# A pre-norm transformer layer on one core: one load, the lead of the row maxima and one bias addition moved by a few slots of a hand-written order

## The chip, the cores and the metric

The kernel runs on one NeuronCore of a Trainium2 chip. The metric is the device time of one execution in microseconds (us). The kernel before takes 2010.45 us, the median of 3 runs from 2010.45 to 2010.8.

## The reference

The input x has the shape (4, 2048, 256) in float32. The layer is attention and then a linear layer, each behind a layer norm and with a residual:

```
x = x + attention(layernorm(x))       # 16 heads of 16, causal, scores / sqrt(256), @ Wo + bo
x = x + linear(layernorm(x))          # weight 256 x 256, + bias
```

In the linear layer both operands are quantised first, in blocks of 32 along a row: each block is divided by its largest magnitude / 7.5, every value goes to the nearest point of the 6-bit grid E2M3, and the block is multiplied by its scale again.

## The kernel before

The tokens are cut into 16 chunks of 512 (four to a batch, n = 0 to 15). The heads are taken in groups of four: 4 batches x 4 groups of heads are 16 groups, and a group has four quarters k = 4g + qc, one for each chunk of 512 queries. A *step* of a quarter is one block of 128 keys against its 512 queries, so the quarters have 4, 8, 12 and 16 steps, a group has 40 and the kernel NS = 640. One *slot* p is the time of one step. Every engine runs a program of its own, in order, and the engines meet only at semaphores; each program is a loop over the same slots, from -20 to about 653.

In slot p TensorE (PE) computes the scores of step p for four heads (`scores`, split in four strips of 32 columns by `by_columns`, L1447), ScalarE (ACT) takes their exponential (L1031), GpSimd (POOL) masks the triangle of a step on the diagonal (`mask`, L840), and PE multiplies by the values two slots later (`values`, L1488). The diagonal steps come early in a quarter and are narrower: 512, 384, 256 and 128 columns.

The exponential needs the maximum of each row beforehand. So PE computes the scores of a quarter once more, ahead of time and the other way round (`unit`, L1447 too): 128 queries against up to 512 keys, into a ring of four PSUM banks, which VectorE (DVE) reduces (`take_unit`, L1189; on the diagonal the masked form of L1184). `max_steps_until(p)` says how many steps of maxima are done by slot p: in the steady part it is p + `MAX_LEAD`, with a ramp in the opening. When a quarter's maxima are all there (slot `MAX_DONE[k]`), four operations follow, a slot apart: `maximum` on DVE (L1196), `split_max` on POOL (L877 to L881, in three bfloat16 parts), `turn_max` on SP (L687, a DMA transpose) and `load_max` on SP (L694, three DMAs into rows 96 to 98 of `q_rows`, so that the score matmul subtracts the maximum itself). The quarter's first score waits for these rows.

Around this stand two other kinds of work, both put into slots by a planner of a few lines at the head of the file. `put` takes the first slot from p on in which the engine has room, by costs written at each call.
- *Projection* of a chunk (`place_early` for chunks 0 to 3, `place_project` for the others, which starts at slot 160 b + 4 + 30 c): `load_x` brings 512 KB of x, DVE takes statistics, POOL (for chunks 0 to 3 DVE) normalises, PE transposes and multiplies by Wq, Wk, Wv, POOL splits Q and K in three bfloat16 parts (L861 to L869), SP stores them to HBM (`store_qk`, four a chunk, numbered r = 4n + m; `store_v`). `load_rows(g, c)` then brings a chunk's rows of Q and K for one group with twelve DMAs of 64 KB (L674), once the four stores of that chunk are in. Chunk 4's `load_x` is followed on SP by `load_later_weights`: Wo, the linear layer's weight and the two biases broadcast over the partitions, four DMAs of 256, 256, 128 and 128 KB.
- *Output* of a chunk, in two halves a = 0, 1 (`place_output`), once all four groups of heads of its batch are done: SP loads the sums (`load_ctx`), the inverses of the denominators (`load_inverse`) and x (`load_again`, 512 KB, L768). POOL adds the first bias to x (`add_mid_bias`, L893) and multiplies the sums by the inverses (`weigh`, L888), PE multiplies by Wo (`attend`), DVE adds the result to x (L1229), and a chain of norm, block maxima, rounding and the second matmul (`feed`) follows. The last four chunks ("late", `quick`) are not weighed but turned on PE (`turn_ctx`).

The order within one slot is fixed in each engine's loop. On SP it is `turn_max`, `load_max`, `store_ctx`, `store_qk`, `store_v`, `load_x`, `load_rows`, `load_values`, and then the output's DMAs, `load_again` last. On POOL it is `mask`, `split_max`, the projection's work, then `weigh` and the output's other work, with `add_mid_bias` last. DVE takes the slot's maxima in four shares with the projection's and the output's work between them.

Of the kernel before, what the change touches and what calls it, by code (L numbers as in the profile page):

```python
# [19 lines left out]
QC = C // CHUNK  # L20
# [36 lines left out]
FIRSTS = [sum(SIZES[:k]) for k in range(NK)]  # L57
# [24 lines left out]

COLUMNS = 32
PRO = 20
MAX_LEAD = 21
SLOTS = range(-PRO, NS + 200)


def max_steps_until(p):

    if p < 0:
        return max(0, min(4, 2 * (p + PRO - 11))) + max(0, min(8, 2 * (p + PRO - 15)))
    if p < 7:
        return 12 + (p + 1) * 12 // 7
    if p < 20:
        return 24 + (p - 6) * 17 // 13
    return min(NS, p + MAX_LEAD)


UNITS_AT = {p: [n for m in range(max_steps_until(p - 1) if p > -PRO else 0, max_steps_until(p))  # L100
                for n in UNIT_STEPS[m]] for p in SLOTS}
MAX_DONE = [min(p for p in SLOTS if max_steps_until(p) >= FIRSTS[k] + SIZES[k]) for k in range(NK)]


# [22 lines left out]
def spend(engine, p, cost):  # L127
    FILLED[engine, p] = FILLED.get((engine, p), 0) + cost
# [10 lines left out]
def item(p, cost, *what):  # L139
    return put("items", p, cost, *what)  # L140


def vector(p, cost, *what):
    return put("vector", p, cost, *what)


def pool(p, cost, *what):
    return put("pool", p, cost, *what)


def sync(p, kind, *which):
    AT.setdefault((kind, p), []).append(which)
# [7 lines left out]
def late(n):  # L160

    return n >= NCH - QC
# [23 lines left out]


def place_project(n, start):
    sync(start - 6, "load_x", n)
    p = vector(start + 1, 0.85, "stats", n, 0)  # L190
    p = vector(p, 0.85, "stats", n, 1)
    p = vector(p, 0.65, "moments", n)
    p = pool(p + 1, 1.0, "deviation", n)
    for a in range(2):
        p = pool(p, 1.2, "normal", n, a)
    p += 1
    for e in range(EH):
        p = item(p, 0.45, "turn_x", n, e)
    p += 2
    lows = []  # L200
    for m, j in ((0, None), (1, 0), (2, None), (3, 1)):

        p = item(max(p, lows[m - 2] if m > 1 else p), 1.75, "project", n, m)
        r = 4 * n + m
        q = pool(p + 2, 1.7, "split", r)
        q = pool(q, 1.7, "split_low", r)
        lows.append(q)
        sync(q + 1, "store_qk", r)
        if j is not None:
            p = item(p + 1, 1.75, "project_v", n, j)  # L210
        p += 1
    sync(max(p, q) + 1, "store_v", n)
    return max(p, q) + 1


def after(p):

    return p + 1 if p < TAIL else p
# [6 lines left out]
def in_order(stage, p):  # L225
    return max(p, STAGE.get(stage, p))


def by_rows(k):


    return k < NK - QC * QC


def place_output(n, a, p):

    quick = late(n)

    def by_vector(p, cost, kind):
        STAGE[kind] = vector(in_order(kind, p), cost, kind, n, a)  # L240
        return STAGE[kind]

    def by_pool(p, cost, kind):
        STAGE[kind] = pool(in_order(kind, p), cost, kind, n, a)
        return STAGE[kind]

    def by_items(p, cost, kind):
        STAGE[kind] = item(in_order(kind, p), cost, kind, n, a)
        return STAGE[kind]

    mid_biased = by_pool(p, 1.35, "add_mid_bias")
    p = by_items(p, 0.45, "turn_ctx") if quick else by_pool(p, 1.3, "weigh")
    p = by_items(max(p + 1 + (p < TAIL), mid_biased), 1.95, "attend")
    spend("vector", p + 1, 0.7)
    p = by_vector(p + 1, 0.85, "stats2")
    p = by_vector(p, 0.35, "moments2")
    p = by_pool(after(p), 1.0, "deviation2")
    p = by_vector(after(p), 1.0, "quick_normal2") if quick else by_pool(p, 1.2, "normal2")
    p = by_vector(p if quick else p + 1, 0.65, "block_max")
    p = by_vector(p, 0.4, "scale")  # L260
    p = by_vector(p, 0.6, "quick_divide") if quick else by_pool(p + 1, 1.3, "divide")
    p = by_vector(p if quick else p + 1, 0.4, "exponent")
    p = by_vector(p, 0.4, "shift_high")
    p = by_vector(p, 0.4, "shift_low")
    q = by_pool(after(p), 1.35, "odd")
    q = by_pool(q, 1.35, "odd_back")
    if quick:
        p = by_vector(p, 0.6, "quick_even")
        p = by_vector(p, 0.6, "quick_even_back")
    else:  # L270
        q = by_pool(q, 1.35, "even")
        q = by_pool(q, 1.35, "even_back")
    p = by_vector(max(p, after(q)), 0.6, "grid")
    p = by_vector(p, 0.6, "quick_dequantise") if quick else by_pool(p + 1, 1.3, "dequantise")
    out_biased = by_pool(q if quick else p, 1.35, "add_out_bias")
    p = by_items(after(p), 0.45, "turn_xd")
    p = by_items(max(p + 1 + (p < TAIL), out_biased), 1.95, "feed")
    spend("vector", p + 1, 0.7)
    sync(p + 2, "store_out", n, a)
    return p + 2  # L280
# [28 lines left out]
for k in range(NK):  # L309
    p = vector(MAX_DONE[k], 0.3, "maximum", k)  # L310
    p = pool(p + 1, 0.9, "split_max", k)
    sync(p + 1, "turn_max", k)
    sync(p + 2, "load_max", k)
    assert p + 4 <= FIRSTS[k] or k < 1, (k, p, FIRSTS[k])
    done_at = FIRSTS[k] + SIZES[k] + 1
    if by_rows(k):
        STORED[k] = p = done_at + 1
        sync(p, "store_ctx", k)
        if k // QC % QC == QC - 1:
            n = k // (QC * QC) * QC + k % QC  # L320
            sync(p + 2, "load_den", n)
            p = vector(p + 7, 0.6, "invert", n) + 1
            sync(p, "store_inverse", n)
            INVERTED[n] = p
        continue
    TURNED[k] = item(done_at + 1, 0.45, "turn_acc", k)
    spend("vector", TURNED[k] + 1, 0.7)
    if k < NK - QC:
        STORED[k] = TURNED[k] + 2
        sync(STORED[k], "store_ctx", k)  # L330
# [4 lines left out]
for b in range(B):  # L335
    if b + 1 < B:
        for c in range(QC):
            n = QC * (b + 1) + c
            PROJECTED[n] = place_project(n, 160 * b + 4 + 30 * c)
            assert PROJECTED[n] + 3 < 160 * b + 138 + 6 * c, (n, PROJECTED[n])  # L340
    for c in range(QC):
        n = QC * b + c
        k = (QC * (b + 1) - 1) * QC + c
        before, times = before_in_set(n)
        free = 0
        if before is not None:
            free = DONE_AT[before] + 1
        elif out_set(n) == 1:
            free = max(PROJECTED.values()) + 2
        if late(n):  # L350
            load = max(STORED[k - QC] + 2, NS - GROUP_STEPS + 2 if before is None else READ_AT[before] + 2)
            ready = max(TURNED[k] + 1, load + 2)
        else:
            load = max(INVERTED[n] + 2, free)
            sync(load, "load_inverse", n)
            ready = load + 5
        sync(load, "load_ctx", n)
        sync(max(load, free), "load_again", n)
        ready = max(ready, free)
        ends = [place_output(n, a, ready) for a in range(2)]  # L360
        READ_AT[n], DONE_AT[n] = STAGE["turn_ctx" if late(n) else "attend"], ends[-1]
for g in range(NG):
    for c in range(QC):
        p = max(GROUP_STEPS * (g - 1) + (8 if g == 1 else 2) + 3 * c, -PRO)
        n = QC * (g // QC) + c
        p = max(p, PROJECTED[n] + 1)
        sync(p, "load_rows", g, c)
        sync(max(p, GROUP_STEPS * (g - 1) + 5 + 3 * c), "load_values", g, c)
p = 36
for step in range(6):  # L370
    p = vector(p, 1.4, "weights", step)
# [1263 lines left out]
```

## Time and profile before

| | |
|---|---|
| median of 3 runs | 2010.45 us |
| the profiled execution | 2009.58 us |
| its span in the trace | 2007.6 us |
| slots 0 to 639 (first score to last) | 95.3 to about 1950 us, some 2.9 us a slot |
| busy share PE, DVE, ACT, POOL | 93%, 85%, 67%, 45% |
| mean granted clock of TensorE | 0.979 |

The page gives the busy time of each engine, the span in 40 slices, the chain of work that ended last and the costliest groups of instructions. The views of the trace used below are the list of waits (which engine waited for which, in total), the timelines of single engines, the chain in order of time, and the busy time by stretches. "[6.57 <-DMA k_rows]" at an instruction means that its engine sat idle for 6.57 us before it and that this transfer ended the wait. SPq is SP's queue of DMA issues. The granted clock is 1.00 at 2.4 GHz and 0.50 at 1.2 GHz.

### The profile page before, as it was taken

How to read it: one execution, taken by the hardware profiler on the slowest of the kernel's cores; microseconds unless marked ns; L12 is line 12 of the kernel's file. 1: busy time of each engine (PE TensorE's matmuls, PEld its weight loads, DVE VectorE, ACT ScalarE, POOL GpSimd, SP SyncE). 2: the span in 40 equal slices, each digit the busy share in tenths (PEclk: the TensorE clock that was granted, in tenths of full speed). 3: DMA queues.
4: the chain of work that ended last, by engine and by line, in shares of the span. 5: the costliest groups of instructions: out<-in, count | busy, mean ns of one | idle time of the engine just before them, and what ended most of it. 6: DMA issues, size and time to landing. Idle time of an engine off the chain costs nothing.

```text
span 2007.6 us, 72033 instructions
## 1 busy us (share of the span) xinstructions
PE 1865.3 (93%) x30053; PEld 801.3 (40%) x30053; DVE 1709.2 (85%) x4334; ACT 1337.6 (67%) x2817; POOL 897.6 (45%) x1187
## 2 busy tenths in 40 slices
PE   6689999999999999999999999999999999999883
PEld 2234444344334443444334343444434444444432
DVE  4697987979988979888897988888999999999976
ACT  5356676777766767677676767666766666777660
POOL 4323334232446546565254646555354654411343
PEclk9899999999999999999999999999999999999996
DMA  5433141414041231503323151331514040131000
GB/s 162 130 85 104 42 114 40 111 52 127 22 125 60 72 107 53 170 18 85 97 59 108 47 153 45 80 117 33 151 42 131 13 110 28 54 86 33 3 33 22
DMA packets 173621, 156.73 MB, mean 78 GB/s; under 512 B 43248, under 2 KB 161008, under 8 KB 173296
## 3 DMA queue, kind: packets, MB, share of 16 engines
q1 hardware_dynamic: 173296, 152.13, 26.9%
q8 instruction: 236, 3.87, 0.8%
q14 instruction: 89, 0.73, 0.1%
HBM read 92.14 MB, written 57.02 MB: 74 GB/s over the span
## 4 chain that ended last, share of the span: by engine, by line
PE 51%; DVE 29%; issue 5%; SPq 4%; POOL 4%; DMA 4%; ACT 2%; POOLq 0%; DVEq 0%; ACTq 0%
PE psum L1447 36%; DVE max_parts L1189 15%; PE psum L1488 13%; DVE psum L1184 6%; SPq L674 3%; ACT probs L1031 2%; DMA out_shop<-in_L_attn_x 1%; DVE max_parts L1184 1%; PE psum L1515 1%; DMA max_rows<-neg_max 1%; PE psum L1507 1%; DVE stats L1248 1%; DVE block_max L1319 1%; POOL out_shop L924 1%; DMA k_rows<-qk_scratch 1%
## 5 line engine op out<-in xcount | busy, mean ns | idle before, releaser
L1031 ACT ACTIVATE probs<-psum 128x512 f32<-128x512 f32 (+3 forms) x2560 | 1204.2, 539 | 422.4 <-PE psum L1447 407.4
L1189 DVE TENSOR_REDUCE max_parts<-psum 128x1 f32<-128x512 f32 x1536 | 956.3, 680 | 96.4 <-PE psum L1447 91.7
L1447 PE MATMUL psum<-q_rows,k_rows 99*32 99x512 bf16 (+3 forms) x10240 | 886.7, 351 | 17.8 <-ACT probs L1031 7.6
L1447 PE MATMUL psum<-k_rows,q_rows 96*32 96x512 bf16 (+3 forms) x10240 | 848.5, 352 | 56.3 <-DVE max_parts L1189 17.4
L1488 PE MATMUL psum<-probs,v_in 128*17 128x512 f32 (+3 forms) x5120 | 587.0, 533 | 4.4 <-POOL probs L840 4.0
L1184 DVE CUSTOM_DVE_ANT_0 psum<-psum,causal 128x128 f32<-128x128 f32 (+3 forms) x1024 | 475.0, 518 | 111.8 <-PE psum L1447 107.9
L1447 PEld LDWEIGHTS psum<-k_rows,q_rows 96*32 96x32 bf16 x10240 | 273.1, 97 | 451.5 <-DVE max_parts L1189 170.3
L1447 PEld LDWEIGHTS psum<-q_rows,k_rows 99*32 99x32 bf16 x10240 | 275.2, 96 | 427.9 <-ACT probs L1031 226.8
L840 POOL TENSOR_SCALAR_AFFINE_SELECT probs<-probs 128x512 f32<-128x512 f32 x256 | 165.9, 648 | 581.5 <-ACT probs L1031 580.5
L1488 PEld LDWEIGHTS psum<-probs,v_in 128*17 128x17 f32 x5120 | 143.3, 98 | 93.4 <-POOL probs L840 5.5
L1184 DVE DVE_READ_ACCUMULATOR2_ANT max_parts<- 128x1 f32 x1024 | 143.4, 140 | 0.0
L877 POOL CAST neg_max<-neg_rest 128x16 bf16<-128x16 f32 x64 | 12.9, 201 | 160.3 <-DVE neg_rest L1196 139.7
L1055 ACT COPY shop<-psum 128x512 f32<-128x512 f32 x56 | 32.9, 587 | 74.4 <-PE psum L1447 74.4
L893 POOL TENSOR_TENSOR out_shop<-out_shop,biases 128x512 f32<-128x512 f32 x48 | 63.2, 1318 | 34.3 <-DMA out_shop<-in_L_attn_x 34.2
L869 POOL TENSOR_TENSOR shop<-shop 128x512 bf16<-128x512 f32 x56 | 65.6, 1171 | 4.6
L1447 PE MATMUL psum<-shop,w_q 128*32 128x512 f32 x512 | 64.6, 632 | 1.6 <-DVE max_parts L1189 0.7
L1447 PE MATMUL psum<-w_v,shop 128*32 128x256 f32 x1024 | 62.9, 387 | 0.6 <-DVE max_parts L1184 0.4
L1447 PE MATMUL psum<-shop,w_k 128*32 128x512 f32 x512 | 60.8, 592 | 0.9 <-DVE max_parts L1184 0.6
L1229 DVE TENSOR_TENSOR out_shop<-psum,out_shop 128x512 f32<-128x512 f32 x48 | 33.1, 691 | 32.0 <-PE psum L1447 31.6
L950 POOL TENSOR_TENSOR out_shop<-out_shop 128x512 f32<-128x512 f32 x24 | 31.9, 1328 | 61.5 <-DVE out_shop L1355 61.5
L853 POOL TENSOR_SCALAR shop<-shop,moments,inv_dev 128x256 f32<-128x256 f32 x48 | 58.8, 1235 | 0.8
L862 POOL TENSOR_TENSOR shop<-shop 128x512 f32<-128x512 f32 x48 | 56.2, 1172 | 4.0
(150 smaller groups left out, 1229.4 us busy)
## 6 DMA issues: line engine op xcount, KB each, us to landing
q_rows<-qk_scratch SPq DMA_DIRECT2D x384, 64.0 KB, 2.6
k_rows<-qk_scratch SPq DMA_DIRECT2D x384, 64.0 KB, 2.6
qk_scratch<-shop SPq DMA_DIRECT2D x56, 384.0 KB, 3.2
sums_scratch<-acc_sb SPq DMA_DIRECT2D x48, 256.0 KB, 2.3
shop<-in_L_attn_x SPq DMA_DIRECT2D x19, 512.0 KB, 4.5
v_scratch<-shop SPq DMA_DIRECT2D x16, 544.0 KB, 4.3
v_in<-v_scratch SPq DMA_DIRECT2D x64, 136.0 KB, 2.5
out_shop<-in_L_attn_x SPq DMA_DIRECT2D x12, 512.0 KB, 7.9
```

The costliest lines, as they stand in the source:

```text
L674: sp.dma_start(dst, src[i if which else l]).then_inc(kq_loaded[u][c], 16)
L840: nc.gpsimd.affine_select(out=tri, in_=tri, compare_op=ALU.is_ge, fill=0.0, base=0, pattern=[[0, HG], [1, P]], channel_multiplier=-1).then ...
L853: ins = nc.gpsimd.tensor_scalar(x_in[n % 2][:, j, :], x_in[n % 2][:, j, :], moments[:, j, 0:1], inv_dev[:, j:j + 1], ALU.subtract, ALU.mult)
L862: nc.gpsimd.tensor_tensor(out=proj[v], in0=proj[v], in1=parts[v][:, 0, :], op=ALU.subtract).then_inc(rest_ready, 1)
L869: nc.gpsimd.tensor_tensor(out=parts[v][:, 2, :], in0=proj[v], in1=parts[v][:, 1, :], op=ALU.subtract).then_inc(low_ready, 1)
L893: return nc.gpsimd.tensor_tensor(out=mine, in0=mine, in1=biases[:, i:i + 1, :].broadcast_to([P, 2, E]), op=ALU.add)
L1031: nc.scalar.activation(probs[s % NPROBS][:, h, a:CHUNK], bank[SCORE_BANKS[n % 3]][:, a:CHUNK], ACT.Exp, scale=SCALE).then_inc(probs_ready, 1)
L1184: ins = nc.vector.tensor_tensor_reduce(out=mine, in0=mine, in1=causal[:, CHUNK - width:CHUNK], scale=1.0, scalar=LOWEST, op0=ALU.add, op1= ...
L1189: nc.vector.tensor_reduce(max_parts[k % 2][:, first:first + heads, t % TILES, c], ring_bank(UNIT_USE[n])[:, 0:heads * width] .rearrange("p ...
L1229: nc.vector.tensor_tensor(out=mine, in0=ring_bank(ITEM_USE[what, n, a]) .rearrange("p (j e) -> p j e", e=E), in1=mine, op=ALU.add).then_in ...
L1447: ins = nc.tensor.matmul(out[r:r + COLUMNS], weights[:, r:r + COLUMNS], moving, start=start, stop=stop)
L1488: ins = nc.tensor.matmul(psum[32 * h:32 * h + VW, ACC_BANK, a:CHUNK], v_in[u][:, kb, h * VW:(h + 1) * VW], probs[s % NPROBS][:, h, a:CHUNK ...
```

## The change

- `MAX_LEAD` goes from 21 to 23, and the ramp of the opening from 17/13 to 18/13 steps a slot so that it meets it. With it the assertion asks for six slots, not four, from a quarter's `split_max` on, except in the first group.
- `place_project` puts `load_x` no earlier than slot 2. Only chunk 4 was earlier (slot -2).
- `place_output` puts, for the chunks that are not late, `weigh` first and `add_mid_bias` two slots behind it. It was the other way round, with both asked for from the same slot on.

```diff
-MAX_LEAD = 21
+MAX_LEAD = 23
...
     if p < 20:
-        return 24 + (p - 6) * 17 // 13
+        return 24 + (p - 6) * 18 // 13
     return min(NS, p + MAX_LEAD)
...
 def place_project(n, start):
-    sync(start - 6, "load_x", n)
+    sync(max(start - 6, 2), "load_x", n)
...
-    mid_biased = by_pool(p, 1.35, "add_mid_bias")
-    p = by_items(p, 0.45, "turn_ctx") if quick else by_pool(p, 1.3, "weigh")
+    if quick:
+        mid_biased = by_pool(p, 1.35, "add_mid_bias")
+        p = by_items(p, 0.45, "turn_ctx")
+    else:
+        p = by_pool(p, 1.3, "weigh")
+        mid_biased = by_pool(p + 2, 1.35, "add_mid_bias")
     p = by_items(max(p + 1 + (p < TAIL), mid_biased), 1.95, "attend")
...
-    assert p + 4 <= FIRSTS[k] or k < 1, (k, p, FIRSTS[k])
+    assert p + (4 if k < QC else 6) <= FIRSTS[k] or k < 1, (k, p, FIRSTS[k])
```

## Rows read from the trace of the kernel before

**Rows 1.** The page: engines' busy us, share, instructions; the chain's shares by engine:
```profile
PE 1865.3 (93%) x30053; PEld 801.3 (40%) x30053; DVE 1709.2 (85%) x4334; ACT 1337.6 (67%) x2817; POOL 897.6 (45%) x1187
PE 51%; DVE 29%; issue 5%; SPq 4%; POOL 4%; DMA 4%; ACT 2%; POOLq 0%; DVEq 0%; ACTq 0%
```

**Rows 2.** Slots 120 to 159: engines in turn, granted clock, DMA share, GB/s:
```profile
450.60:469.80 19.20, 18.75 (x328) 7.61 (x324) 18.01 (x43) 14.88 (x35) 4.61 (x10) 1.00 0.35 87
469.80:495.70 25.90, 25.64 (x452) 11.03 (x448) 25.90 (x59) 20.21 (x48) 3.82 (x6) 1.00 0.58 152
495.70:551.40 55.70, 53.23 (x896) 21.40 (x892) 50.92 (x152) 41.11 (x84) 24.05 (x34) 1.00 0.12 34
```

**Rows 3.** Waits over the span: us in total, times, longest us:
```profile
POOL out_shop L893 <- DMA out_shop<-in_L_attn_x: 34.2, 6, 8.1
PEld psum L1447 <- DMA k_rows<-qk_scratch: 17.3, 3, 7.1
PE psum L1447 <- DMA q_rows<-max_rows: 5.7, 3, 3.7
PE psum L1488 <- POOL probs L840: 4.0, 2, 2.3
```

**Rows 4.** SP's timeline, opening: start us, duration us, what is issued:
```profile
87.36 0.49 SPq L645 DMA_DIRECT2D shop<-in_L_attn_x  x1
90.24 1.26 SPq L674 DMA_DIRECT2D q_rows<-qk_scratch  x3
112.34 0.42 SPq L674 DMA_DIRECT2D k_rows<-qk_scratch  x1
```

**Rows 5.** Chain of waits, opening: start us, duration us, what:
```profile
69.00 2.55 DMA k_rows<-qk_scratch
95.37 6.13 DMA k_rows<-qk_scratch
```

**Rows 6.** Timelines of PE and DVE, opening; idle time before in brackets:
```profile
101.55 0.62 PE L1447 MATMUL psum<-k_rows,q_rows 96*32 96x512 bf16 x4 [6.57 <-DMA k_rows<-qk_scratch]
121.97 0.75 DVE L1248 BATCH_NORM_STATS2 stats<-shop 128x6 f32<-128x256 f32 x2
130.41 0.69 DVE L1189 TENSOR_REDUCE max_parts<-psum 128x1 f32<-128x512 f32 x1
```

**Rows 7.** Twelve heads on the chain; masked maxima by shape (busy, mean ns):
```profile
470.38 7.12 DVE max_parts L1189 x12
L1184 DVE CUSTOM_DVE_ANT_0 psum<-psum,causal 128x512 f32<-128x512 f32 x256 | 170.2, 718 | 14.8 <-PE psum L1447 13.8
L1184 DVE CUSTOM_DVE_ANT_0 psum<-psum,causal 128x128 f32<-128x128 f32 x256 | 66.7, 322 | 46.0 <-PE psum L1447 45.7
```

**Rows 8.** Chain of waits: 13 heads on PE; one step of values:
```profile
730.67 2.84 PE psum L1447 x52
853.60 0.86 PE psum L1488 x8
```

**Rows 9.** Around slot 304: PE's timeline, the chain, POOL's timeline:
```profile
982.54 0.40 PE L1447 MATMUL psum<-q_rows,k_rows 99*32 99x512 bf16 x4 [3.69 <-DMA q_rows<-max_rows]
972.68 6.78 DMA max_rows<-neg_max
977.83 1.28 POOL L893 TENSOR_TENSOR out_shop<-out_shop,biases 128x512 f32<-128x512 f32 x1 [5.18 <-DMA out_shop<-in_L_attn_x]
```

**Rows 10.** Busy time by stretch around one wait for a mask:
```profile
850.00:852.00 2.00, 2.00 (x28) 0.96 (x32) 0.80 (x2) 0.56 (x2) 2.00 (x2) 0.50 0.34 119
852.00:854.00 2.00, 2.00 (x28) 0.73 (x20) 1.90 (x5) 1.20 (x2) 2.00 (x3) 0.67 0.00 1
844.00:848.00 4.00, 3.78 (x68) 1.44 (x59) 3.96 (x12) 3.23 (x8) 0.00 (x0) 1.00 1.04 347
```

**Rows 11.** Chunk 3's first addition: the chain, POOL's timeline:
```profile
839.32 8.55 DMA out_shop<-in_L_attn_x
848.01 1.26 POOL L893 TENSOR_TENSOR out_shop<-out_shop,biases 128x512 f32<-128x512 f32 x1 [7.60 <-DMA out_shop<-in_L_attn_x]
```

## The prediction

> **What bounds the kernel now.** I read the busy shares first: PE is busy 93% of the span and DVE 85% [rows 1]. The chain that ended last splits 51% PE, 29% DVE, 4% DMA, 4% POOL [rows 1]. So PE sets the pace, DVE takes it over in places, and a few waits for transfers stand between. In slots 120 to 159, a group of 40 slots with little other work, the three stretches of slots 0-7, 8-19 and 20-39 of the group show where which engine leads: in the middle one DVE is busy for all 25.9 us; in the last one it has 4.8 us to spare [rows 2]. Next the list of waits over the whole span [rows 3]: PE's weight loads wait 17.3 us for the rows of K (three times), its matmuls 5.7 us for the rows of the maxima and 4.0 us for masks, and POOL sits 34.2 us before the first bias's addition. POOL's idle time counts only where PE waits for a mask that stands behind it. The change touches exactly these three, and shifts the maxima against the scores.
>
> **Part 1, the load of chunk 4.** `load_x(4)` is the only one that moves: its slot was 4 - 6 = -2 and becomes 2; for the others start - 6 is far over 2. With it go the four DMAs of `load_later_weights`. On SP the five are issued from 87.36 on, and at 90.24 the twelve DMAs of `load_rows(0,2)` follow [rows 4]. The chain of waits names the landing of a store as what released the rows at 90.24. But that store is r = 13, of chunk 3, and `load_rows(0,2)` waits only for r up to 11; SP simply issues without a gap, so the five cost their issue time, 90.24 - 87.36 = 2.9 us. Their bytes cost as much again: the last K row of chunk 2 takes 6.13 us to land, where the same DMA of chunk 1 took 2.55 [rows 5]. PE sits 6.57 us for it [rows 6]. Without the five in front the row lands 2.9 + 3.6 = 6.5 us sooner, near 95.0, when PE has just come there; I take 6.4, all on the path, since DVE then runs without a gap for 40 us. Bounds: 0 (were the chain right, and the stores what makes the landing slow) and 7.0 (DVE's gap too).
> The load now passes the stores of r = 14 and 15, `turn_max(1)`, `store_v(3)` and `load_max(1)`, and stands before `load_rows(0,3)`. SP issued the last DMA of `load_rows(0,3)` at 112.34 [rows 4]. Five issues (2.9 us) and a landing 3.6 us longer put its end at 112.3 + 2.5 + 6.5 = 121.3 at the latest. The first maxima that need chunk 3 are taken by DVE at 130.41, now 124.0, so the cover is at least 2.7 us, and more by what SP too comes sooner; the statistics of chunk 4 at 121.97, now 115.6, need x that would be issued by 106 and even with 6 us lands before [rows 6]. I take nothing for either; if the cover were gone, what is late would come off the 6.4.
>
> **Part 2, the lead.** Two steps more by slot 20, and the last two slots with maxima (618 and 619) become free. Two early steps (256 and 384 columns, four heads) are 1.1 us on PE (2.5 x 4 x 0.215 / 2) or 3.6 on DVE (4 x 0.38 + 4 x 0.52 [rows 7]); two of 512 columns at the end are 1.7 us on PE (8 x 0.215 [rows 8]) or 5.0 on DVE (4 x 0.59 + 4 x 0.65). PE on both sides: -0.6. Bounds +1.9 and -3.9.
> *The wait for the rows of maxima.* It falls on the first slot of a group's last quarter, where only four slots stand between the last maxima and the first use. At slot 304 PE waits 3.69 us [rows 9], at slots 144 and 624 the other 2.0 of its 5.7 [rows 3]. After a wait of this kind PE runs at half the clock for a while: behind the mask's wait at 849.9 the granted clock is 0.50 (1.2 GHz) for 2 us and 0.67 for 2 more, 1.0 + 0.66 = 1.7 us lost [rows 10]; the same is lost behind slot 304. With two slots more (4.3 us, a sixth of the 25.9 us that 12 slots take) the first idea is that all of it goes, 5.7 us and 1.7 of clock, 7.4. The rows speak against that for slot 304. The transpose issued at 972.68 lands 6.78 us later, at 979.46; x of `load_again(4)`, issued 2.7 us before it, lands just before POOL's addition at 977.83 [rows 9]: the transpose is held by what was issued ahead, not only by the late maximum. `load_again(4)` is in slot 136 of its batch and still ahead of `turn_max`. Issued as soon as x is, at 970.9, the transpose lands after x all the same, near 978.2, and the wait falls by 1.3 us, not by 3.7, and the clock falls as before.
> The Trainium skill, page "DMA: Bandwidth & Descriptors", section "Queues, rings and completion order", says the same in general: the increment of a DMA's semaphore lands only after every earlier write of that DMA engine. By that rule a transpose behind x can't report before x; without it the gain at slot 304 would be the whole 3.7 and 1.7 of clock, and the sum would be 4.1 us lower, an estimate from the rows.
> I take 1.3 at slot 304, the 2.0 of the other two and 0.3 for what its weight loads lose besides: -3.6. Bounds 0 and -7.4.
> *How maxima and scores stand beside each other.* DVE needs for a head of 512 columns 0.59 us (12 in 7.12), for a masked one of 512 columns 0.65 and of 128 0.25 (0.07 less than the means, since starts overlap), for 384 and 256 columns 0.52 and 0.38 between them [rows 7]. PE needs 0.215 us for a head of 512 columns of scores or maxima (13 in 2.84, less a little), and 0.86 for a step of values [rows 8], less in proportion on the diagonal. Summed over a group by the kernel's own lists of steps, slots 0-7, 8-19, 20-39: lead 21 PE 17.2, 25.4, 45.1 and DVE 18.0, 26.4, 41.9; lead 23 PE 17.2, 24.7, 45.8 and DVE 18.0, 25.1, 43.1. The larger of the two in each stretch sums to 89.5 before and 88.9 after: 0.6 us a group, because full steps of maxima leave the short diagonal slots in the middle. The trace agrees on which engine leads where [rows 2]. Over 14 groups 8.4 us; projections and output work fill many of these gaps, so I take half, -4.2. Bounds: -8.4, and +14.4, if the 1.2 us more of DVE in slots 20-39 counts in full in the 12 groups that have output work.
>
> **Part 3, the first bias's addition.** For chunks 0 to 11 `weigh` now comes first and the addition two slots later. The addition is what waits for x, six times, 34.2 us. PE feels two of them, 4.0 us for masks, the longer 2.3 [rows 3]: for chunk 3 near 849.9 and, in the same place of the next batch, for chunk 7. POOL shows why: the addition starts at 848.01 after 7.60 us idle and takes 1.26 [rows 11], and the mask comes behind it. Both are followed by the low clock, 1.7 us each [rows 10]. Now `weigh` stands there and waits for the sums and the inverses, issued just ahead of x, which is issued at 839.32 and lands 8.55 us later [rows 11]. The trace doesn't show when they land. The 512 KB of x at the 347 GB/s of 844-848 take 1.5 us [rows 10], so at least that much earlier. The waits are 1.7 and 2.3, so at most 0.2 and 0.8 us stay, and I take both as gone: 4.0 + 3.4 = -7.4. Bounds 0 and -7.9 (0.5 that the weight loads wait besides). Nothing is added: the same 24 additions, and DVE's addition of `attend` waits for them as before.
>
> **Sum.** -6.4 - 0.6 - 3.6 - 4.2 - 7.4 = -22.2. The profiled execution took 2009.58 (span 2007.6 and 2.0 around it), so 1987.4; it lay 0.9 below the median of the runs, 2010.45, so 1988 in the runs.
>
> **Rivals.**
> *A, the waits only change their name.* `weigh` waits for the same full queue and the masks behind it with it, of the waits for the maxima's rows only 2.1 go, and the pairing gives nothing: -6.4 - 0.6 - 2.1 = -9.1, 2001. For it: 1 MB lies ahead of x in the same queue. Against it: PE needs only 2 us.
> *B, slower: DVE waits for the late addition.* `attend` is now two slots behind `weigh`, and DVE, in order, takes it one slot later and needs the addition. From `weigh` that is one slot (2.5) and the matmuls of `attend` (1.7), 4.2 us; POOL has the other half's `weigh` to do (the addition's kind and shape, 1.3 [rows 11]), a mask (0.65 on the page) and the addition, 3.2 us. It decides once one more POOL instruction of over 1.0 us stands between, as parts of the splits do (1.17 on the page). Everything behind on DVE, the maxima, then waits, and PE after four banks. At a whole addition for each of 24 halves: 24 x 1.28 = 30.7 on top of the sum, 2019.
> *C, all of it comes*: -7.0 - 3.9 - 7.4 - 8.4 - 7.9 = -34.6, 1976. For it: every term is a wait or a surplus that the rows show. Against it: the transpose behind x.
> *D, the gains are taken back*: what PE no longer waits for a transfer it waits for DVE, which is busy 85% itself [rows 1], or the change doesn't reach the waits at all: 2009.5 to 2010.5. Against it: PE's own idle time shows them.
>
> **Numbers.** Forecast 0.45, C 0.20, A 0.15, B 0.10, D 0.10. A measurement tells about 0.2% (4 us) from no change. Faster: 0.45 + 0.20 + 0.15 = 0.80; same 0.09; slower 0.11. The range reaches over A and to C and leaves B and D out: 1975 to 2006. The forecast's own is 1981 to 1997.
>
> **What would show it.** The last K row of chunk 2 lands near 95.0, in about 2.5 us, and PE's gap of 6.6 us before it is gone. `load_rows(0,3)` makes nobody wait. POOL's waits for x before the addition are gone or short, `weigh` has some of them, and no wait of PE for a mask stays, nor half clock behind it. At slot 304 a wait of 2 us or more for the maxima's rows stays with the transpose landing right after x; if it is gone, my reading of the queue is wrong. A group of 40 slots with little other work takes about 0.6 us less than 100.8. DVE waiting for POOL's addition would be B.

## The result: slower, not faster

The changed kernel takes 2018.8 us, the median of 11 runs, against 2007.3 for the kernel before on the same chip. The ratio is 1.0048, with a 95% interval from 1.0033 to 1.0064: +9.6 us, where -22 was forecast. The profiled execution took 2017.14 us with a span of 2015.4, 7.6 us more than that of before (2009.58). A profile shows one execution, and those of one kernel differ by up to 20 us here (2007.3 is the middle of 1998.0 to 2018.1), so the traces tell where time goes, and only the medians how much.

### The profile page after: what moved, and what is told of

Read it like the earlier page. It is cut to its first block, busy times and chain, and to the rows that moved or that the text cites. A ratio compares the mean times of both kernels' runs of the same rounds, so it can differ in the third digit from the quotient of the medians.

```text
span 2015.4 us, 72025 instructions
## 1 busy us (share of the span) xinstructions
PE 1869.2 (93%) x30053; PEld 804.0 (40%) x30053; DVE 1715.4 (85%) x4334; ACT 1332.4 (66%) x2817; POOL 892.8 (44%) x1187
## 4 chain that ended last, share of the span: by engine, by line
PE 60%; DVE 23%; issue 5%; ACT 5%; DMA 2%; SPq 2%; POOL 2%; POOLq 0%; DVEq 0%; ACTq 0%
PE psum L1452 42%; PE psum L1493 16%; DVE max_parts L1194 10%; DVE psum L1189 5%; ACT probs L1036 3%; SPq L679 2%; ACT acc_sb L1045 1%; DMA max_rows<-neg_max 1%; DVE max_parts L1189 1%; PE psum L1520 1%; PE psum L1512 1%; DVE out_shop L1355 1%; DVE block_max L1324 0%; DMA qk_scratch<-shop 0%; DVE stats L1253 0%
## 5 line engine op out<-in xcount | busy, mean ns | idle before, releaser
L1452 PE MATMUL psum<-q_rows,k_rows 99*32 99x512 bf16 (+3 forms) x10240 | 892.5, 351 | 26.8 <-ACT probs L1036 17.5
L1452 PE MATMUL psum<-k_rows,q_rows 96*32 96x512 bf16 (+3 forms) x10240 | 851.7, 351 | 42.4 <-DVE max_parts L1194 14.9
L1493 PE MATMUL psum<-probs,v_in 128*17 128x512 f32 (+3 forms) x5120 | 590.2, 533 | 13.9 <-POOL probs L845 9.6
L1452 PEld LDWEIGHTS psum<-q_rows,k_rows 99*32 99x32 bf16 x10240 | 278.2, 96 | 461.5 <-ACT probs L1036 249.2
L1452 PEld LDWEIGHTS psum<-k_rows,q_rows 96*32 96x32 bf16 x10240 | 273.2, 97 | 411.5 <-DVE max_parts L1194 146.6
L845 POOL TENSOR_SCALAR_AFFINE_SELECT probs<-probs 128x512 f32<-128x512 f32 x256 | 166.4, 650 | 589.3 <-ACT probs L1036 589.0
L1493 PEld LDWEIGHTS psum<-probs,v_in 128*17 128x17 f32 x5120 | 143.3, 98 | 102.0 <-POOL probs L845 11.9
L882 POOL CAST neg_max<-neg_rest 128x16 bf16<-128x16 f32 x64 | 12.7, 198 | 146.6 <-DVE neg_rest L1201 135.5
L1452 PE MATMUL psum<-shop,w_q 128*32 128x512 f32 x512 | 66.1, 644 | 0.7 <-ACT shop L1049 0.7
L1452 PE MATMUL psum<-shop,w_k 128*32 128x512 f32 x512 | 61.7, 593 | 1.8 <-DVE max_parts L1189 1.1
L898 POOL TENSOR_TENSOR out_shop<-out_shop,biases 128x512 f32<-128x512 f32 x48 | 62.7, 1314 | 0.2 <-DMA out_shop<-in_L_attn_x 0.2
L1452 PE MATMUL psum<-w_v,shop 128*32 128x256 f32 x1024 | 61.9, 382 | 1.0 <-DVE max_parts L1194 0.6
```

The costliest lines, as they stand in the source:

```text
L845: nc.gpsimd.affine_select(out=tri, in_=tri, compare_op=ALU.is_ge, fill=0.0, base=0, pattern=[[0, HG], [1, P]], channel_multiplier=-1).then ...
L898: return nc.gpsimd.tensor_tensor(out=mine, in0=mine, in1=biases[:, i:i + 1, :].broadcast_to([P, 2, E]), op=ALU.add)
L1452: ins = nc.tensor.matmul(out[r:r + COLUMNS], weights[:, r:r + COLUMNS], moving, start=start, stop=stop)
L1493: ins = nc.tensor.matmul(psum[32 * h:32 * h + VW, ACC_BANK, a:CHUNK], v_in[u][:, kb, h * VW:(h + 1) * VW], probs[s % NPROBS][:, h, a:CHUNK ...
```

## The profile after

All lines behind the planner stand five further down: L1447 is L1452, L1488 is L1493, L840 is L845, L674 is L679. Mind L893: it was the first bias's addition, and is now `weigh`; the addition is L898.

The page first (engines' busy us and shares; the chain's shares), beside [rows 1]:

```profile
PE 1869.2 (93%) x30053; PEld 804.0 (40%) x30053; DVE 1715.4 (85%) x4334; ACT 1332.4 (66%) x2817; POOL 892.8 (44%) x1187
PE 60%; DVE 23%; issue 5%; ACT 5%; DMA 2%; SPq 2%; POOL 2%; POOLq 0%; DVEq 0%; ACTq 0%
```

Nothing there says slower. The list of waits does (us in total, times, longest), beside [rows 3]:

```profile
POOL out_shop L893 <- DMA out_shop<-inverse_scratch: 64.9, 7, 15.0
PEld psum L1452 <- DMA k_rows<-qk_scratch: 11.3, 3, 5.4
PE psum L1493 <- POOL probs L845: 9.6, 6, 4.7
PE psum L1452 <- DMA q_rows<-max_rows: 6.0, 2, 3.6
```

PE's weight loads wait 6.0 us less for rows of K; PE waits as long as before for the maxima's rows, and 5.6 us more for masks. POOL, which sat 34.2 us before the addition, sits 64.9 us before the weighing.

*The opening came as forecast.* The timelines of PE and SP, with `load_x(4)` and the last row of chunk 3 [rows 4, 6]:

```profile
96.15 0.40 PE L1452 MATMUL psum<-k_rows,q_rows 96*32 96x512 bf16 x4 [0.26 <-DMA k_rows<-qk_scratch]
...
103.11 0.59 SPq L650 DMA_DIRECT2D shop<-in_L_attn_x  x1
...
112.04 0.43 SPq L679 DMA_DIRECT2D k_rows<-qk_scratch  x1
```

And the landing of chunk 2's last K row in the chain [rows 5]:

```profile
93.52 2.59 DMA k_rows<-qk_scratch
```

It lands at 96.1, not 101.5 (95.0 was forecast), and the gap of 6.57 us is 0.26. Slot 12 begins at 137.7, not 143.4.

*Then it is lost, in several places.* A slot begins here with its first exponential on ACT. Counted so, the changed kernel takes 3.7 us more than before in slots 20 to 39, 3.0 in 120 to 139, 2.8 in 300 to 319 and 6.2 in 460 to 479. Slots 240 to 279 take 8.0 us less, but 280 to 299 take 9.7 more, because the planner has moved work from the former to the latter; from 260 to 299 the net is 3.4 more, and in their copy, 420 to 459, 4.0. Slots 200 to 219 and 360 to 379 take 5.4 and 5.2 more, of which 3.2 come back each time in the next 20.

The longest waits for a mask stand in those last two stretches, at slot 218 and its copy in the next batch, 378: slots 211 to 239 take 93.9 us, before 89.3. SP's timeline ahead of it in the changed kernel (start, duration, what is issued):

```profile
706.57 2.96 SPq L679 DMA_DIRECT2D q_rows<-qk_scratch  x3
...
713.32 0.43 SPq L679 DMA_DIRECT2D k_rows<-qk_scratch  x1
713.85 0.37 SPq L686 DMA_DIRECT2D v_in<-v_scratch  x1
714.31 1.36 SPq L740 DMA_DIRECT2D out_shop<-sums_scratch  x2
715.77 1.21 SPq L767 DMA_DIRECT2D out_shop<-inverse_scratch  x2
717.02 0.47 SPq L773 DMA_DIRECT2D out_shop<-in_L_attn_x  x1
```

The same x in the kernel before:

```profile
716.99 0.45 SPq L768 DMA_DIRECT2D out_shop<-in_L_attn_x  x1
```

Both belong to slot 211. That slot begins at 698.5 after and at 704.3 before. PE had gained 5.8 us by then, and SP nothing: it is 18.5 us behind the slot instead of 12.7. Among what it has to issue first are, at 704.82 and 705.29, the last two stores of chunk 8, which the planner has moved from slot 192 to 209. What follows on POOL and PE:

```profile
723.77 1.26 POOL L893 TENSOR_TENSOR out_shop<-out_shop 128x512 f32<-128x512 f32 x1 [13.89 <-DMA out_shop<-inverse_scratch]
724.99 0.64 POOL L845 TENSOR_SCALAR_AFFINE_SELECT probs<-probs 128x512 f32<-128x512 f32 x1
...
725.68 1.05 PE L1493 MATMUL psum<-probs,v_in 128*17 128x256 f32 x8 [3.51 <-POOL probs L845]
```

And the busy time by stretch (length; PE, PEld, DVE, ACT, POOL; granted clock, DMA share, GB/s):

```profile
724.00:728.00 4.00, 2.32 (x40) 1.34 (x44) 0.58 (x5) 0.45 (x2) 3.77 (x8) 0.60 0.35 128
728.00:732.00 4.00, 4.00 (x48) 1.87 (x44) 1.23 (x7) 0.69 (x2) 3.92 (x5) 0.54 0.05 9
```

POOL waits 13.9 us for the inverses, the mask stands behind `weigh`, and PE waits 3.5 us for it. It starts again at 725.68 and works at a granted clock of 0.50 (1.2 GHz) until 731.7, which costs 6.0 / 2 = 3.0 us more; the 0.60 above is a mean with PE's idle time before 725.68 in it. One wait of 3.5 costs 6.5. The wait that the change removed at chunk 3 [rows 10, 11] has come back a chunk earlier, twice as long.

## The experiments

Medians in us, with the ratio to the kernel before (run beside it each time) and its interval.

| kernel | median | ratio | 95% |
|---|---|---|---|
| e1 load only | 2001.5 | 0.9966 | 0.9946 to 0.9986 |
| e2 lead only | 2028.7 | 1.0101 | 1.0075 to 1.0126 |
| e3 bias only | 2004.2 | 0.9987 | 0.9970 to 1.0003 |
| e4 lead and bias | 2024.3 | 1.0076 | 1.0050 to 1.0101 |
| e5 load and bias | 2003.0 | 0.9974 | 0.9963 to 0.9985 |
| e6 maxima early | 2024.4 | 1.0078 | 1.0056 to 1.0099 |
| e7 places only | 2034.4 | 1.0125 | 1.0105 to 1.0145 |
| e8 lead 22 | 2033.9 | 1.0123 | 1.0104 to 1.0142 |
| e9 late projections | 2010.8 | 1.0015 | 1.0003 to 1.0028 |
| e10 lead, early projections | 2029.1 | 1.0110 | 1.0093 to 1.0127 |
| e11 lead, rows spaced | 2015.0 | 1.0034 | 1.0019 to 1.0049 |
| e12 load, rows spaced | 1995.0 | 0.9943 | 0.9923 to 0.9962 |
| e13 the change, rows spaced | 2002.1 | 0.9975 | 0.9960 to 0.9991 |
| e14 load and bias, rows spaced | 1999.6 | 0.9961 | 0.9943 to 0.9980 |
| e15 load, rows 4 apart | 1998.8 | 0.9955 | 0.9935 to 0.9975 |

**Which part.** e1 to e4 are the diff's parts: e1 the line of `load_x`, e2 `MAX_LEAD` and the ramp, e3 the block of `place_output`, e4 the last two together. e5 has all but the lead.

> Only the load of chunk 4 moves. In the changed kernel slot 1 came 6.8 us sooner, and by slot 21 only 4.3 us of it were left. Theory T (the load is a gain, something else in the change is the loss): 3 to 7 us faster than before, PE's gap before the maxima of chunk 2 gone (6.6 to about 0), and the gain lasts past slot 21, since no maxima are added there. Rival R1 (an opening gain is taken back later by transfers or DVE whatever else is changed): less than 1.5 us faster.

> Only the lead goes to 23, with its ramp. Theory L (the planner moves projections and output work when the maxima move, and the new places are worse): 5 to 12 us slower than before, spread over the groups that have projections and output work. Rival W (the loss sits in weigh standing first, before the inverses land): no slower than before, -8 to 0 us, as the prediction's own terms say (-0.6 - 3.6 - 4.2).

> Only weigh first and the first bias's addition two slots later. Rival W: 8 to 15 us slower than before, POOL idle before weigh for the inverses 50 us or more in total and PE waits for masks of 4 us or more in each of two places. Theory L: -4 to +2 us; POOL's idle time for the inverses near the 34 us that it had for x, and PE's waits for masks at most the 4.0 us of before.

> The change without the moved load. If the load is worth what the opening showed, this is 3 to 7 us slower than the whole change, so 12 to 17 us slower than before. If the lead and the bias add up, it is the sum of the two kernels that have them alone; theory X (each is harmless alone, but together slot 216 comes 7 us sooner against loads that are issued no sooner, so POOL waits 14 us with a mask behind it): both alone within 4 us of before, this one 10 us or more slower, with the waits of 3.5 and 4.7 us for masks at slots 218 and 378 in this kernel and in neither of the other two.

> The kernel before with the load of chunk 4 and the first bias's addition moved, the lead left at 21. Theory L (the loss is all the lead's; the other two add up): -6.8 of the load alone and -2.6 of the bias alone, so 2008.6 - 9.4 = 1999, ratio 0.995. Rival X (the parts disturb each other, since the load and the addition change what POOL and SP do at other places): not faster than the load alone, 2001.5 or more, ratio 0.9966 or above.

By the ratios the load brings -6.8, the bias -2.6, the lead +20.3; the sum is +10.9, the whole change +9.6. So the lead is the whole loss. e2 is slower than either of its two cases had it, and e4 (+15.3) fell where the load's gain put it. e5, 5.2 us faster than before, falls on the rival's side by its number, but its interval overlaps that of the load alone: beside the load, the bias brings nothing that can be told.

**The lead itself, or the places that the planner finds with it?** With a lead of 23 the planner also puts the other work elsewhere: DVE's room in a slot hangs on `UNITS_AT`, and `split_max` takes POOL's room two slots earlier. Worked out from `put` for the lead alone, the last store of chunk 8's projection goes from slot 192 to 208, of chunk 9's from 229 to 245, of chunk 10's from 255 to 270. e6 keeps all places and moves only the maxima and their four operations; e7 keeps those (but for three quarters late in the kernel, where they lie a slot earlier) and moves the rest; e8 is one lead in between.

```
 # e6: behind the planner, which has run with a lead of 21
+MAX_LEAD, RAMP = 23, 18
+UNITS_AT = {...}; MAX_DONE = [...]
+...   (takes the old entries of the four kinds out of the plan)
+for k in range(NK):
+    for i, kind in enumerate(("maximum", "split_max", "turn_max", "load_max")):
+        sync(MAX_DONE[k] + i, kind, k)
 # e7: the same lines with 21, 17, behind a planner that has run with 23
 # e8
-MAX_LEAD = 21
+MAX_LEAD = 22
```

> The plan of the kernel before is kept slot by slot for projections, output work and loads; only the steps of maxima, maximum, split_max, turn_max and load_max take the places that a lead of 23 gives them. Nothing is left out. Theory P (what costs is that the planner, seeing the maxima two slots earlier, puts projections and output work elsewhere, at 214-216 instead of 211-215 and so on): about 2008.6 less what the wait for the rows of maxima brings, -3 to -6, so 2003 to 2006. Rival M (what costs is the maxima themselves beside the scores, as the 1.2 us more of DVE in slots 20-39 of a group): most of the 20 us of the lead alone, 2020 to 2029.

> The reverse: steps of maxima, maximum, split_max, turn_max and load_max stay where a lead of 21 has them; projections and output work lie where the planner puts them for a lead of 23. Theory P: nearly all the loss of the lead alone, 2022 to 2030. Rival M: near the kernel before, 2006 to 2012. If each does half, both kernels lie near 2018 and the two costs are independent.

> Lead 22 instead of 21, the early steps as before. The short (masked) steps of maxima now stand beside the short steps of scores instead of beside the long ones. If the loss of the lead grew with its size (theory of a smooth cost, rival M in its simple form): half of 20, 2018. If it hangs on where the planner puts the work (theory P): anything, since the places change again. If the pairing of short with long was worth what the sums over a group say, it is slower than both neighbours: over 2029.

Neither theory holds alone: +16 and +25 can't be halves of +20. Each of the two loses by itself. For e6 the trace shows one place: the planner had fitted the maxima's operations and the rest round each other, and now `split_max(11)`, `deviation` and a `normal` stand together in slot 98, and PE waits 4.3 us for the mask behind them at slot 101; slots 100 to 119 take 8.4 us more. (The profiled execution of e6, 2015.96, is its fastest, 8.5 us under its median, so the trace doesn't hold the whole loss.) So these kernels price a misfit too, not the lead alone. That lead 22 is as slow as 23 says that the cost does not grow with the lead. The number lies where the pairing's case put it, but the planner has moved the other work here as well, so that doesn't show the pairing.

**The end of the projections?** The whole difference in e9 and e10 is the start of the projections of batches 2 and 3.

```
-            PROJECTED[n] = place_project(n, 160 * b + 4 + 30 * c)
+            PROJECTED[n] = place_project(n, 160 * b + (5 if b else 4) + 30 * c)   # e9; e10: 3, with the lead of 23
```

> The kernel before (lead 21) with the start of the projections of batches 2 and 3 one slot later (5 instead of 4), batch 1 as it was. The planner's first-fit then ends chunk 8 at slot 208 instead of 192 and chunk 9 at 238 instead of 229 (12 and 13 likewise), as it does, nearly, for a lead of 23 (208 and 245); maxima and output work stay in their slots. Theory Q (the lead costs because first-fit lets the projections end up to 16 slots later, so that SP issues their stores and the rows behind them just ahead of the loads of x): slower by 6 to 15 us, 2015 to 2024. Rival M2 (the ends of the projections don't matter; what costs is the maxima's chain among the masks and normals of POOL): 2006 to 2011.

> Lead 23 as in the lead alone, with the start of the projections of batches 2 and 3 one slot earlier (3 instead of 4): chunks 8 and 12 end at 195 and 355 instead of 208 and 368; chunk 9 stays at 245. Theory Q: part of the 20 us comes back, 4 to 10, so 2019 to 2025. Rival M2: as the lead alone, 2026 to 2030.

A miss. Chunk 8 at 208 and chunk 9 at 238 together cost 3 us; chunk 8 back at 195 under the lead of 23 gives nothing. What neither run isolates is chunk 9's last store at slot 245, where the lead puts it, just ahead of `load_rows(7, 1)`.

**SP's lateness.** In e2 SP issues chunk 3's x 19.9 us after its slot, 251, begins at 826.6; before it was 10.0. SP's, POOL's and PE's timelines of e2 there:

```profile
846.46 0.45 SPq L768 DMA_DIRECT2D out_shop<-in_L_attn_x  x1
...
854.17 1.26 POOL L893 TENSOR_TENSOR out_shop<-out_shop,biases 128x512 f32<-128x512 f32 x1 [12.87 <-DMA out_shop<-in_L_attn_x]
...
856.07 1.06 PE L1488 MATMUL psum<-probs,v_in 128*17 128x256 f32 x8 [6.04 <-POOL probs L840]
```

Ahead of it SP issues the rows of four chunks, 48 DMAs, in slots 242 to 251, with the waits for their stores between. They aren't needed until the next group's maxima, from slot 257 on. e11 to e13 spread them:

```
-        p = max(GROUP_STEPS * (g - 1) + (8 if g == 1 else 2) + 3 * c, -PRO)
+        p = max(GROUP_STEPS * (g - 1) + (8 if g == 1 else 2) + 5 * c, -PRO)
```

> Lead 23 as in the lead alone, with the loads of K's and Q's rows of a group's four chunks 5 slots apart instead of 3 (slots 2, 7, 12, 17 of a group instead of 2, 5, 8, 11). All else as in the lead alone. There SP issued x of chunk 3 19.9 us after its slot had begun (10.0 in the kernel before), behind 24 DMAs of rows, and PE waited 13.0 us for masks with the half clock behind it. Theory Q: SP is no longer behind at slot 251, the wait of POOL for x and those of PE for masks are nearly gone, -10 to -16, so 2013 to 2019. Rival M2: SP's lateness isn't what delays the masks, 2025 to 2030.

> The load of chunk 4 moved as in the change, lead 21, the addition in its old place, and the rows' loads 5 slots apart. The candidate for a kernel faster than both. Theory Q: the load's -7 and the two waits for masks with their low clock (4.0 + 3.4), so 1992 to 1996. Rival: the load's alone, 2001; or slower than that, if rows that come later make maxima wait.

> The changed kernel, whole, with the rows' loads of a group 5 slots apart instead of 3. In the changed kernel SP issued x of chunk 2 18.5 us after its slot had begun (12.7 in the kernel before) and POOL's weighing waited 64.9 us for the inverses, PE 9.6 us for masks. Theory Q (SP's lateness is what the change brought): these waits go, 13 to 17 us less than the changed kernel's 2018.8, so 2002 to 2006. Rival (the new order on POOL, weighing first, or the placements themselves cost): 2010 or more.

The medians of all three lie where theory Q said. e2 and e11 in the list of waits, e2 first:

```profile
POOL out_shop L893 <- DMA out_shop<-in_L_attn_x: 24.9, 2, 12.9
PE psum L1488 <- POOL probs L840: 13.0, 5, 6.0
```

```profile
POOL out_shop L893 <- DMA out_shop<-in_L_attn_x: 7.4, 3, 3.5
PE psum L1488 <- POOL probs L840: 1.7, 3, 1.3
```

e11's gain over e2 by slot 639 is 11.9 us: 8.5 and 7.7 are gained in the groups of slots 240 and 400, where these waits were, and 4.3 are lost again elsewhere. In e13 the x of slot 211 is issued at 700.74, 5.7 us behind its slot, and the weighing there waits 5.1 us, with no long wait for a mask behind it (timelines, then waits):

```profile
700.74 0.38 SPq L773 DMA_DIRECT2D out_shop<-in_L_attn_x  x1
...
711.48 1.27 POOL L893 TENSOR_TENSOR out_shop<-out_shop 128x512 f32<-128x512 f32 x1 [5.07 <-DMA out_shop<-inverse_scratch]
```

```profile
POOL out_shop L893 <- DMA out_shop<-inverse_scratch: 37.1, 6, 9.7
PE psum L1493 <- POOL probs L845: 1.4, 4, 0.9
```

So one line turns the change from +9.6 to -5.0; against the changed kernel, e13's trace gains 6.1 and 6.3 us in slots 200 to 219 and 360 to 379, and 3.7 in 120 to 139. It also has 37 us of POOL's waiting beside 1.4 us of PE's: the sum of a wait off the path says little.

The line helps without the lead too, so the comparison that isolates the lead is the one at equal spacing, with load and addition moved in all four kernels. With the rows 3 slots apart the lead costs 0.0074 in the ratio, 14.9 us (e5 to the change). With 5 slots it costs 0.0014, 2.8 us (e14 to e13, whose intervals overlap). So about 12 of the 15 us appear only when the lead meets an SP that is late, give or take some 6 by the intervals.

> Lead 21, the load and the addition moved, the rows' loads 5 slots apart. Theory Q: with SP in time the order of addition and weighing is worth nothing, within 3 us of the load with spacing, 1995.0. Rival: the addition's move is worth its 2.6 us still, 1992.

> Lead 21, the load moved, the rows' loads 4 slots apart. With 5, PE waited 10.9 us for the rows of maxima, since load_rows of the last chunk stands just ahead of turn_max at slot 140 of a batch (3.8 us there). With 4 that wait should be near the 5.7 of the kernel before, and if SP is still in time at x (the waits for masks stay at nothing) the time is 1991 to 1994; if 4 isn't enough for x, 1997 to 2001.

e12, the load with rows 5 apart and neither lead nor bias, has the lowest median of all, 1995.0. The spacing brings it 4.6 us over the load alone (e1), with overlapping intervals, and e13, the whole change with spacing, is by the ratios 6.4 us slower than e12. e12's price is a longer wait for the maxima's rows:

```profile
POOL out_shop L893 <- DMA out_shop<-in_L_attn_x: 4.4, 4, 1.7
PE psum L1447 <- DMA q_rows<-max_rows: 10.9, 5, 3.8
```

With 4 slots (e15) that wait falls to 6.5, and POOL's for x is back at 22.9. The median, 1998.8, falls in the second case expected, "4 isn't enough for x"; but the trace has no wait of PE for a mask, which was the first case's sign, so the reason given for the second isn't shown. e14 lies above both of its cases by its median; its interval and e15's overlap that of e12, so neither is told apart from it, and nothing speaks for the bias's move here either.

## Why the prediction was wrong, step by step

**Part 1, the load: right.** -6.4 forecast, -6.8 measured by e1. In the changed kernel 5.7 of it stand at slot 12. The ranking of the reasons (issue time and landing, not the stores) held: the row lands in 2.59 us.

**Part 2, the lead: this failed.** Its three terms sum to -8.4; e2 measured +20.3. The step at fault is the one that priced the lead as "two steps more by slot 20" and a shift of maxima against scores, with all other work where it was. The planner reads both of the things that the lead moves; the slots of the projections and of the output had to be worked out anew, and weren't. The terms themselves:
- *Ramp and end*, -0.6. The early steps cost DVE's price, not PE's: slots 20 to 39 go from 48.6 us to 52.3 in the profile of e2 as of e11, and e6, which has the early steps without the new places, takes 3.3 us more in slots 0 to 39. Slots 600 to 639 give back 3.5 and 2.5. The net is +0.2 to +1.2, inside my bounds. Not in my sum at all was the tail from slot 639 on, 61.3 us in the changed kernel for 58.0: its transposes wait otherwise, after first, then before:

```profile
PE psum L1520 <- DVE q_rows L1317: 12.5, 2, 10.3
```

```profile
PE psum L1515 <- issue: 10.0, 1, 10.0
```

e7, with the places alone, has that 12.5; e6, without them, has the 10.0. So it is the places.
- *The maxima's rows*, -3.6. Alone (e2) these waits do vanish, 5.7 us to nothing. In the changed kernel 6.0 stay, at slots 304 and 464. PE's timeline at 304, then the chain, beside [rows 9]:

```profile
988.51 0.40 PE L1452 MATMUL psum<-q_rows,k_rows 99*32 99x512 bf16 x4 [2.43 <-DMA q_rows<-max_rows]
```

```profile
973.05 11.10 DMA max_rows<-neg_max
```

The wait there is 1.26 us less than before, where 1.3 was forecast, but that is luck. The forecast had the transpose land right behind x, which was issued 6.7 us ahead of it. x took 12.8 us and landed at 979.1, and the transpose landed 5.0 us later still, at 984.15. Between the two stand the twelve DMAs of `load_rows(8, 3)`, issued from 966.95 on, the last of which landed at 983.0. The planner had moved them from slot 291 to 297, just behind x, which was in no term of mine. In e2 they stand at slot 301, behind the transpose; that is issued when x has landed, takes 2.2 us, and PE doesn't wait. Nor did the clock fall behind the wait, as I had it: it is 1.00 for the 6 us after 988.51. That a late transpose is held by what was issued ahead of it did hold. The rule of the Trainium skill ("DMA: Bandwidth & Descriptors", section "Queues, rings and completion order"), that a DMA's increment comes after the earlier writes of its engine, agrees.
- *The pairing*, -4.2, or 0.6 a quiet group. Slots 120 to 127, 128 to 139 and 140 to 159, before, after, and in e13 (columns as above):

```profile
450.56:469.81 19.25, 18.80 (x332) 7.61 (x324) 18.06 (x43) 14.94 (x36) 4.61 (x10) 1.00 0.35 87
469.81:497.17 27.36, 27.10 (x480) 11.68 (x476) 27.36 (x64) 21.18 (x51) 3.82 (x6) 1.00 0.60 159
497.17:551.36 54.19, 51.72 (x872) 20.75 (x868) 49.41 (x147) 40.10 (x82) 24.05 (x34) 1.00 0.10 27
```

```profile
446.08:465.20 19.12, 18.58 (x332) 7.71 (x327) 18.39 (x42) 14.62 (x35) 4.59 (x10) 1.00 0.23 66
465.20:495.67 30.47, 28.30 (x488) 12.65 (x484) 26.87 (x70) 21.22 (x50) 4.60 (x10) 0.94 0.62 154
495.67:549.20 53.53, 52.36 (x868) 20.36 (x864) 50.16 (x141) 39.98 (x82) 23.00 (x30) 1.00 0.10 28
```

```profile
446.34:465.45 19.11, 18.57 (x332) 7.55 (x327) 18.40 (x42) 14.62 (x36) 4.58 (x10) 1.00 0.26 73
465.45:492.21 26.76, 26.43 (x488) 11.98 (x483) 26.54 (x70) 21.09 (x50) 5.26 (x11) 1.00 0.65 159
492.21:545.76 53.55, 52.39 (x868) 20.29 (x864) 50.18 (x141) 40.01 (x83) 22.23 (x30) 1.00 0.17 34
```

Undisturbed (e13) the group takes 99.4 us for 100.8, 1.4 less. Of that 0.8 is the wait for the maxima's rows at slot 144, which belongs to the term above; 0.6 are left for the pairing, as summed, but in one group of one execution that is not shown. In the changed kernel the middle stretch has a wait that no rival named, DVE's for the denominators, and the clock falls to 0.94; 3.7 us go there:

```profile
480.45 0.55 DVE L1277 RECIPROCAL den<-den 128x64 f32<-128x64 f32 x1 [1.85 <-DMA den<-sums_scratch]
```

**Part 3, the bias: the waits went, the gain didn't come.** -7.4 forecast, -2.6 measured (e3), with an interval that reaches over no change. Alone, the step "at most 0.2 and 0.8 us stay" held: in e3's trace PE has no wait for a mask, and `weigh` waits 17.1 us for the inverses, 4.5 at the longest. What failed is the sum, which took these waits and their clock for the whole effect. Asked for in the new order, the two operations move other work: worked out from `put`, the loads of chunk 3's sums, inverses and x go from slot 251 to 247, and the last stores of chunks 9 and 10 from 229 and 255 to 241 and 280. In e3's trace slots 240 to 279 take 7.8 us less and slots 280 to 299 take 8.7 more. Which of these moves takes back the gain no run shows.
In the changed kernel the step itself failed as well. It compared the landings of sums, inverses and x, 1.5 us apart, and took SP's issuing as given. But at slot 211 the sums are issued 2.7 us and the inverses 1.3 us before x, all at the end of SP's backlog, and where the slots come earlier they are as late as x was. POOL's longest wait at `weigh` is 15.0 us, where that of the addition was 8.1.

**The rivals.** A, "the waits only change their name", is the one that was nearest, with a chance of 0.15: `weigh` does wait for the same full queue. But A knew no way to be slower than before. B, the slower one, is another mechanism than what happened: at slot 218 DVE does wait 2.4 us for the late addition, but as a consequence of the late weighing. What made the kernel slower, the moved work and above all SP's lateness, is in no rival. The lateness could be seen in the trace of before: x of slot 211 is issued at 716.99, 12.7 us behind its slot.

What stays open: why e2 with the rows spaced (e11) is still 7 us above before. Its profile has 3.2 us more in the early steps, 3.1 in the tail, and 6.5 and 6.8 more in slots 260 to 299 and 420 to 459, against gains elsewhere, but no experiment tells these apart. No run has the kernel before with the spacing alone, and none separates the store at slot 245 from the other places that the lead moves.

## What to carry to other kernels

Where a planner or a greedy placement stands between a constant and the program, compare the placed orders, operation by operation, before pricing the constant. And read the issuing queue as an engine: note, for each load on which others wait, how far behind its place in the order it is issued. In this kernel a queue that was late already gave back none of the time that the engines gained, and its victim was what stood in order behind the one who waited. Spreading issues that nobody needed yet was worth 14.6 us in the changed kernel, more than any part of the change, and 4.6 beside the load alone.

## What the runs showed of the hardware

SP's issuing had the larger share in when x landed: in the changed kernel x of slot 211 was issued 18.5 us after the slot had begun, and landed 7.7 us later. The transfers had a share too. In e13 the same x was issued 5.7 us after its slot, but with DMAs of rows right behind it, from 701.30 on, instead of ahead, it took 13.1 us to land.

The twelve DMAs of a chunk's rows and the load of its values hold SP from 706.57 to 714.22, 7.7 us, though the median landing of the former is 2.6 to 2.7 us. The Trainium skill, "DMA: Bandwidth & Descriptors", section "Issuing engines are not separate DMA queues", calls the time of issue "usually small relative to the DMA itself". For DMAs of 64 KB it was 0.45 us each (0.9 for two), a sixth of the landing, and at times more: the first three here took 2.96 us. With 48 of them in ten slots x was issued 10.0 us behind its slot before, and 19.9 in e2.

The clock: the wait of 3.5 us was followed by 6.0 us at 0.50 (1.2 GHz), 3.0 us lost; the one of 1.8 us before the change by 0.50 and 0.67 over 4 us, 1.7 lost [rows 10]. These two stalls cost PE about twice their length. It is no rule: behind the wait of 2.4 us at slot 304 in the changed kernel the granted clock stayed at 1.00, and the wait of 6.0 us in e2 was followed by 0.50, 0.50 and 0.73 over 6 us, 2.5 lost.
